# Eight gated cross-attention and feed-forward layers on one core: the last stage's experts on seven full tiles instead of eight short ones, two rounds sooner

## The chip, the cores and the metric

One core of one Trainium2 chip runs the whole program in one launch. The metric is device time in microseconds (us), the median of several executions. Engines are called TensorE (PE in the profile, PEld for its weight loads), VectorE (DVE), ScalarE (ACT), GpSimd (POOL) and SyncE (SP).

## What is computed

The reference is a stack of four layers, each a gated cross-attention and a gated feed-forward on x, which has 8 sequences of 112 rows of 1024 values. Only the last layer's two parts bear on the change:

```
idx = top_k(-pdist, 16)                      # 16 nearest of 1024 points, per sequence
gathered = take_along_axis(feat, idx)        # feat: layer norm of x, (1024 points, 112 rows)
x = x + tanh(g_xattn[3]) * (einsum('bkm,k->bm', gathered, affine_w) + affine_b)
# experts, row by row
p = softmax(layernorm(x) @ gate_w.T)         # 8 experts, the best two kept and made to sum to 1
x = x + tanh(g_ffn[3]) * sum_e w[e] * (layernorm(x) @ lora_A[e].T @ lora_B[e].T)
```

The experts treat each row by itself, so rows may be grouped in any way. The gather works on one sequence at a time and needs all its rows.

## The kernel before

The function `gather_experts` (L2829) is the last stage. It starts at about 2477 us. It is written as one list of rounds, `u` from 0 to 161 (`ROUNDS`, L2843). All four compute engines walk the same list in program order, so a wait in one round holds back all later rounds of that engine. A sequence b has 16 rounds, u = 16b to 16b+15, and k is the round's place in it.

In each round VectorE makes a one-hot matrix (`marked(u + 2)`, L3090, two rounds ahead), TensorE multiplies it with the table of the sequence (`looked`, L2938, 24 small matmuls at L2947), and VectorE reduces the result (`kept`, L3098, L3105). Three one-hot buffers and three banks of the look-up tie the two engines together within about three rounds. Every four rounds TensorE turns four results (`turned`, L2951) and ScalarE copies them to `flat` (L3017). Round k = 13 makes the next sequence's table (`tabled`, `split`), rounds 2 to 6 its layer norm.

The results of sequence b then take a path through memory to be regrouped. In round 16(b+1)+1 ScalarE stores `flat` (L3024, 448 KB); in round 16(b+1)+5 ScalarE waits for that store and issues the load into `back` (`back_load`, L3026, 448 KB). In the round that `returns` names (L2882: 16(b+1)+9, for b = 0 16(b+1)+11) TensorE waits for the load and turns the values (`returned`, L2960, L2966). Two rounds later VectorE adds them to x (`update`, L3109, L3114).

The experts of sequence m are 22 steps t, step t in round 16(m+1)+12+t (`steps`, L2877; for m = 0 the first five steps lie in rounds 30 to 32). t = 0 to 3 is the layer norm, t = 5 turns the rows (L2983, L675), t = 7 to 10 are the gate and the first product (L2973, with `zT`: 16 instructions of 128x8 and 16 of 128x512), t = 10 and 11 the weights and h on VectorE, t = 13 turns h, t = 15 to 18 are the second product (L2973, with `hT`, 16 of 128x512), t = 18 and 20 add it to x (L3165), t = 21 stores the rows (L3051). These steps handle 112 rows at a time. All lie in the same rounds as the gather of later sequences; only the last sequence's have nothing beside them.

The queues: SyncE loads the broadcast numbers of the next sequences (L298, 912 KB and 72 KB per piece, four pieces a sequence), each piece as soon as the buffer's rounds are consumed. ScalarE issues all other transfers of the stage: loads of x (L3058, round k = 0), `flat`, `back` and the output. GpSimd does one iota (L2925) and nothing else. Its DMAs are the software_dynamic queue of the profile.

Of the kernel before, what the change touches and what calls it, by code (L numbers as in the profile page):

```python
# [15 lines left out]
U32 = mybir.dt.uint32  # L16
# [2812 lines left out]
def gather_experts(nc, C, banks, gate, gate_ffn, x_in, x_out, A, gather, early):  # L2829
# [13 lines left out]
    ROUNDS = U + 12 + 22  # L2843
    with ExitStack() as ctx:
# [7 lines left out]
        norm = Norm(s_, 4)  # L2852
        shift = s_.sb("shift", [Q, 4, 1])
# [7 lines left out]
        zm, zT = s_.sb("zm", [Q, D]), s_.sb("zT", [P, KC, Q])  # L2861
        prob, best, w8, hit = (s_.sb(n, [Q, NE]) for n in ("prob", "best", "w8", "hit"))
        place, placef, number = s_.sb("place", [Q, 8], U32), s_.sb("placef", [Q, 8]), s_.sb("number", [Q, NE])
        nmax, both = s_.sb("nmax", [Q, 1]), s_.sb("both", [Q, 1])
        h, hT = s_.sb("h", [Q, RE]), s_.sb("hT", [P, RE // P, Q])
# [9 lines left out]
            s_.sem(n) for n in ("zm_ready", "zT_ready", "max_ready", "prob_ready", "h_ready", "hT_ready", "x_done"))  # L2875

        def steps(u):  # L2877
# [8 lines left out]
        order, nth = [], {}  # L2886
        for u in range(ROUNDS):
# [9 lines left out]
            if k == 2 and b + 1 < B:  # L2897
                nth["points", b + 1] = len(nth)
            for m, t in steps(u):
                if t == 0:  # L2900
                    nth["experts", m] = len(nth)
# [11 lines left out]

        @block.sync
        def _(sp):
            sp.wait_ge(x_loaded[2], 16)
            for b in range(1, B):
                for c in range(4):
                    if b >= 2:
                        sp.wait_ge(onehot_ready, (b - 2) * K + 4 * (c + 1))  # L2920
                    gather.load_spread(sp, b, c, spread_loaded[b % 2][c], spread[b % 2])

        @block.gpsimd
        def _(pool):
            pool.iota(number[:], pattern=[[1, NE]], base=0, channel_multiplier=0,  # L2925
                      allow_small_or_imprecise_dtypes=True).then_inc(numbered, 1)

        @block.tensor
        def _(pe):
# [39 lines left out]
            def part_of(t, lhsT, w, ks, n):  # L2969
                if ks[0] == 0:  # L2970
                    pe.wait_ge(turns.free(t), turns.count(t, 0))
                for k in ks:
                    mm = pe.matmul(turns.tile(t)[0:Q, 0:n], lhsT[:, k, :], w(k), start=(k == 0), stop=(k == lhsT.shape[1] - 1))  # L2973
# [3 lines left out]
            def experts(m, t):  # L2977
                if t == 5:
                    if m == 0:
                        pe.wait_ge(early.loaded["gT"], 16)  # L2980
                        pe.wait_ge(gather.weights_loaded, 32)
                    pe.wait_ge(zm_ready, m + 1)
                    turn_rows(pe, C, turns, zm, "zT", m, 0)  # L2983
                if t == 7:
                    pe.wait_ge(zT_ready, m + 1)
# [3 lines left out]
                if t == 13:  # L2989
                    pe.wait_ge(h_ready, m + 1)  # L2990
                    turn_rows(pe, C, turns, h, "hT", m, 0, n=1)
                if t == 15:
                    pe.wait_ge(hT_ready, m + 1)
# [19 lines left out]
        def _(act):  # L3013
            def turned(i):
                t = ("turn", i)
                act.wait_ge(turns.full(t), turns.count(t, 0))
                op = act.activation(flat[:, i // 4 % 2, :, i % 4 * 4:i % 4 * 4 + 4],  # L3017
# [8 lines left out]
            def back_load(b):  # L3026
                act.wait_ge(flat_stored, 16 * b + 16)
                act.dma_start(back[:, b % 2].rearrange("p t f -> p (t f)"),
                              flat_dram[b % 2].rearrange("a c -> (a c)").rearrange("(p c) -> p c", p=P)).then_inc(back_loaded[b % 2], 16)

            def scaled(out, src, i, n, ready):
                act.wait_ge(shift_ready, n + 1)
# [274 lines left out]
```

## Time and profile before

| what | us |
|---|---|
| three runs | 2803.63, 2813.75, 2813.39 (median 2813.39) |
| the profiled execution, its own time | 2815.97 |
| its span, first to last instruction | 2814.3 |
| TensorE busy in the span, from the page | 2584.0 (92%) |
| last stage, from its first look-up at 2477.5 to the end | 336.8 |
| granted clock of TensorE, mean over the span | 0.962 of full speed |

The rows of the trace name a line, an engine, what is written and read, how often, and times in us. A stretch A:B is counted from the span's start. For the last stage two kinds of moments are used as marks below: T_b is when ScalarE issues the store of `flat` of sequence b (2503.91, 2538.12, 2580.22, 2617.76, 2655.56, 2693.13, 2729.39 and 2762.68 for b = 0 to 7), and R_b is when TensorE begins to turn the returned values of b (2520.68, 2559.63, 2598.95, 2636.49, 2673.98, 2710.57, 2746.93 and 2776.40).

### The profile page before, as it was taken

How to read it: one execution, taken by the hardware profiler on the slowest of the kernel's cores; microseconds unless marked ns; L12 is line 12 of the kernel's file. 1: busy time of each engine (PE TensorE's matmuls, PEld its weight loads, DVE VectorE, ACT ScalarE, POOL GpSimd, SP SyncE). 2: the span in 40 equal slices, each digit the busy share in tenths (PEclk: the TensorE clock that was granted, in tenths of full speed). 3: DMA queues.
4: the chain of work that ended last, by engine and by line, in shares of the span. 5: the costliest groups of instructions: out<-in, count | busy, mean ns of one | idle time of the engine just before them, and what ended most of it. 6: DMA issues, size and time to landing. Idle time of an engine off the chain costs nothing. (4 is left out here: it accounts for less than half of the span.)

```text
span 2814.3 us, 48289 instructions
## 1 busy us (share of the span) xinstructions
PE 2584.0 (92%) x18264; PEld 1841.8 (65%) x18268; DVE 1898.8 (67%) x3366; ACT 1080.5 (38%) x2605; POOL 553.1 (20%) x602
## 2 busy tenths in 40 slices
PE   7999999999999699998899999998788999878898
PEld 5856855855865488886555555655487788556664
DVE  6376376376467577774578877777558889867774
ACT  3443434334335233332334444443355655302221
POOL 0110100001012100000045554455223333200000
PEclk9999999999999899998899999998899999989998
DMA  8011010101113845556275666544250010544521
GB/s 325 2 38 58 3 59 23 38 25 58 37 47 82 278 115 140 157 149 220 103 246 165 180 172 172 161 127 118 63 201 9 24 47 24 141 142 169 176 98 33
DMA packets 155491, 311.31 MB, mean 111 GB/s; under 512 B 84112, under 2 KB 107312, under 8 KB 145768
## 3 DMA queue, kind: packets, MB, share of 16 engines
q1 hardware_dynamic: 128952, 232.78, 25.8%
q0 software_dynamic: 20384, 60.82, 7.3%
q10 hardware_dynamic: 5936, 14.75, 1.8%
q8 instruction: 141, 2.31, 0.4%
q14 instruction: 78, 0.64, 0.1%
HBM read 249.53 MB, written 42.52 MB: 104 GB/s over the span
## 5 line engine op out<-in xcount | busy, mean ns | idle before, releaser
L1765 DVE TENSOR_REDUCE latent_nmax<-bank 112x1 f32<-112x487 f32 x128 | 85.0, 665 | 242.9 <-PE bank L1568 236.5
L1460 POOL TENSOR_SCALAR latent_probs<-latent_probs,latent_rsum 112x487 f32<-112x487 f32 x128 | 89.0, 709 | 786.0 <-DVE latent_rsum L1770 786.0
L2197 POOL TENSOR_SCALAR grouped_probs<-grouped_probs,grouped_rsum 112x375 f32<-112x375 f32 x256 | 169.8, 682 | 280.5 <-DVE grouped_rsum L2253 280.4
L2464 PE MATMUL bank<-ffn_qT,gather_whole 128*128 128x128 bf16 x3584 | 207.0, 220 | 16.7 <-ACT ffn_us L2587 6.7
L2464 PEld LDWEIGHTS bank<-ffn_qT,gather_whole 128*128 128x128 fp8e4 x3584 | 203.0, 98 | 21.6 <-issue 20.3
L2647 POOL TENSOR_TENSOR ffn_h<-ffn_sl,ffn_us 128x512 f32<-128x512 f32 x56 | 126.8, 2265 | 278.6 <-ACTq L2590 278.6
L2144 ACT ACTIVATE grouped_probs<-bank,grouped_nmax 112x375 f32<-112x375 f32 x256 | 143.3, 572 | 76.0 <-DVE grouped_nmax L2249 76.0
L2249 DVE TENSOR_REDUCE grouped_nmax<-bank 112x1 f32<-112x375 f32 x256 | 122.3, 540 | 73.4 <-PE bank L2055 71.1
L2947 PEld LDWEIGHTS bank<-gather_part,points_onehot 123*128 123x128 bf16 x3072 | 109.2, 101 | 60.9 <-DVE points_onehot L3095 30.8
L2064 PEld LDWEIGHTS bank<-const_ident,grouped_probs 112*125 112x125 f32 x768 | 105.4, 196 | 66.4 <-DVE grouped_probsT L2261 28.8
L2191 POOL TENSOR_SCALAR grouped_raw<-grouped_raw,grouped_rscale 128x1024 f32<-128x1024 f32 x96 | 119.9, 1270 | 144.7 <-DVEq L2227 144.5
L1515 PE MATMUL bank<-latent_zT,front_wq 128*128 128x224 f32 x768 | 148.0, 353 | 0.0
L1540 PE MATMUL bank<-latent_wo,latent_oT 128*128 128x512 f32 x336 | 146.6, 592 | 0.0
L1515 PEld LDWEIGHTS bank<-latent_zT,front_wq 128*128 128x128 f32 x768 | 145.0, 190 | 1.9 <-issue 1.8
L2947 PE MATMUL bank<-gather_part,points_onehot 123*128 123x63 bf16 x3072 | 115.2, 198 | 27.7 <-DVE points_onehot L3095 24.3
L2064 PE MATMUL bank<-const_ident,grouped_probs 112*125 112x112 f32 x768 | 110.2, 283 | 23.7 <-DVE grouped_probsT L2261 18.8
L1475 PE MATMUL bank<-front_wkv,front_cT 128*125 128x384 f32 x384 | 127.3, 492 | 0.0
L1475 PE MATMUL bank<-front_cT,front_wkv 128*128 128x375 f32 x384 | 123.3, 478 | 0.0
L1700 ACT ACTIVATE latent_probs<-bank,latent_nmax 112x487 f32<-112x487 f32 x128 | 85.5, 668 | 91.2 <-DVE latent_nmax L1765 80.9
L2580 ACT ACTIVATE ffn_sl<-ffn_gs,ffn_sgu 128x128 f32<-128x128 f32 x224 | 71.6, 390 | 116.5 <-DVEq L2710 116.0
L1527 PE MATMUL bank<-latent_probsT,latent_v 125*96 125x224 f32 (+1 forms) x512 | 110.1, 358 | 4.0 <-DVEq L1784 4.0
L1540 PEld LDWEIGHTS bank<-latent_wo,latent_oT 128*128 128x128 f32 x336 | 63.2, 190 | 73.9 <-issue 73.7
(435 smaller groups left out, 5561.7 us busy)
## 6 DMA issues: line engine op xcount, KB each, us to landing
grouped_raw<-L_weights SPq DMA_DIRECT2D x24, 2048.0 KB, 8.9
points_spread<-numbers SPq DMA_DIRECT2D x16, 912.0 KB
codes<-grouped_flip SPq DMA_DIRECT2D x24, 512.0 KB, 2.6
front_cT<-ctxT SPq DMA_DIRECT2D x8, 1500.0 KB, 6.8
plain_ctxT<-ctxT POOLq DMA_DIRECT2D x8, 1500.0 KB, 22.2
plain_ctx<-ctx POOLq DMA_DIRECT2D x8, 1500.0 KB, 23.5
grouped_ctx<-ctxT SPq DMA_DIRECT2D x8, 1500.0 KB, 6.8
gather_whole<-numbers SPq DMA_DIRECT2D x12, 912.0 KB
```

What stands on the lines that cost most here:

```text
L1475: mm = pe.matmul(turns.tile(t)[0:m, 0:n], lhsT(k), rhs(k), start=(k == 0), stop=(k == KC - 1))
L1515: mm = pe.matmul(turns.tile(t)[:, c * 2 * Q:(c + 1) * 2 * Q], wq[:, k, (2 * i + c) * P:(2 * i + c + 1) * P], zT[:, k].rearrange("p s q -> ...
L1527: mm = pe.matmul(turns.tile(t)[0:HD, 2 * half * Q:2 * (half + 1) * Q], v[0:n, k, g * HD:(g + 1) * HD], pT[0:n, half, k], start=(k == 0), s ...
L1540: mm = pe.matmul(turns.tile(t)[:], oT[:, (b - 1) % 2, k, :], wo[:, k, i * 512:(i + 1) * 512], start=(k == 0), stop=(k == OC - 1))
L2064: mm = pe.transpose(turns.tile(t)[0:CT, j * Q:(j + 1) * Q], pr[:, g % 2, j, k * CT:(k + 1) * CT], C.ident[0:Q, 0:Q])
L2144: act.activation(pr[:, i, j, :], turns.tile(t)[0:Q, 0:CTX], ACT.Exp, bias=nmax[:, i, j:j + 1], accum_out=rsum[:, i, j:j + 1]).then_inc(tur ...
L2191: pool.tensor_scalar(w, w, rscale[:, slot, i % m:i % m + 1], MAGIC, ALU.mult, ALU.add).then_inc(raw_scaled, 1)
L2197: pool.tensor_scalar(pr[:, g % 2, j, :], pr[:, g % 2, j, :], rsum[:, g % 2, j:j + 1], 1.0, ALU.mult, ALU.mult)\
L2249: dve.tensor_reduce(nmax[:, g % 2, j:j + 1], turns.tile(t)[0:Q, 0:CTX], AX, ALU.max, negate=True).then_inc(max_ready, 1)
L2464: mm = pe.matmul(ahead.tile(t)[:, i * P:(i + 1) * P], wgu[:, u0 + f // 4, c:c + 2 * P - 1:2], qT[:, k, :], start=(k == 0), stop=(k == KC - 1))
L2647: pool.tensor_tensor(h[:, G * j:G * j + G, :], sl[:, j % 2], us[:, j % 2], ALU.mult).then_inc(h_ready, 1)
L2947: mm = pe.matmul(turns.tile(t)[:, j * RA:(j + 1) * RA], onehot[0:ROWS, u % 3, j * P:(j + 1) * P], part[n][0:ROWS, b % 2, :], start=(n == 0 ...
```

## The change

Sequences 1 to 7 have 112 rows each, on partitions 0 to 111 of their tile. The 112 rows of sequence 0 are cut into seven parts of 16, and each part is copied onto partitions 112 to 127 of one of these tiles (`full[m]`). The experts run for m = 1 to 7 on 128 rows; m = 0 has none. `returns` goes from round 16(b+1)+9 to 16(b+1)+7 (b = 0 stays at +11), the experts from 16(m+1)+12+t to 16(m+1)+10+t. The load of `back` goes from ScalarE's queue to GpSimd's, where it stands in no round but behind the store of `flat` alone. GpSimd also copies the seven parts (after `update(0)`, semaphore `first_done`; VectorE waits for them, `rows_moved`, in step 0 of m = 1) and stores the 16 extra rows of each tile, the last one excepted, which SyncE stores.

```diff
-    ROUNDS = U + 12 + 22
+    ROUNDS = U + 10 + 22
-        rest_x, z = s_.sb("x", [Q, B - 1, D]), s_.sb("z", [Q, 2, NA * CH])
-        x = [early.sb["x0"][:]] + [rest_x[:, b, :] for b in range(B - 1)]
+        rest_x, z = s_.sb("x", [P, B - 1, D]), s_.sb("z", [Q, 2, NA * CH])
+        x = [early.sb["x0"][:]] + [rest_x[0:Q, b, :] for b in range(B - 1)]
+        full = [None] + [rest_x[:, b, :] for b in range(B - 1)]
...
-            return [(m, t) for m in range(B) for t in range(22)
-                    if u == ((30, 30, 31, 31, 32)[t] if m == 0 and t < 5 else 16 * (m + 1) + 12 + t)]
+            return [(m, t) for m in range(1, B) for t in range(22) if u == 16 * (m + 1) + 10 + t]
...
-            return [m for m in range(B) if u == 16 * (m + 1) + (11 if m == 0 else 9)]
+            return [m for m in range(B) if u == 16 * (m + 1) + (11 if m == 0 else 7)]
...
+        def back_load(eng, b):
+            eng.wait_ge(flat_stored, 16 * b + 16)
+            eng.dma_start(back[:, b % 2].rearrange("p t f -> p (t f)"),
+                          flat_dram[b % 2].rearrange("a c -> (a c)").rearrange("(p c) -> p c", p=P)).then_inc(back_loaded[b % 2], 16)
+
+        def store_first(eng, m, stored):
+            eng.dma_start(x_out[0][(P - Q) * (m - 1):(P - Q) * m], full[m][Q:P]).then_inc(stored, 16)
...
+            sp.wait_ge(x_done, B - 1)
+            store_first(sp, B - 1, x_stored)
...
+            back_load(pool, 0)
+            pool.wait_ge(first_done, 1)
+            for m in range(1, B):
+                pool.dma_start(full[m][Q:P], x[0][(P - Q) * (m - 1):(P - Q) * m]).then_inc(rows_moved, 16)
+            for b in range(1, B):
+                back_load(pool, b)
+                if b >= 3:
+                    pool.wait_ge(x_done, b - 2)
+                    store_first(pool, b - 2, rows_stored)
+            pool.wait_ge(x_done, B - 2)
+            store_first(pool, B - 2, rows_stored)
+            pool.wait_ge(rows_stored, 16 * (B - 2))
...
+                if i % 4 == 0 and i >= 8:
+                    act.wait_ge(flat_stored, 16 * (i // 4 - 1))
...
-                if k == 5 and 1 <= b <= B:
-                    back_load(b - 1)
...
-                dve.drain()
+                if b == 0:
+                    dve.drain().then_inc(first_done, 1)
+                else:
+                    dve.drain()
...
+                    if m == 1:
+                        dve.wait_ge(rows_moved, 16 * (B - 1))
+                    wide.statistics(dve, full[m], i)
```

The rest of the diff widens the experts' tiles from 112 to 128 partitions, gives them a layer-norm workspace of their own (`wide`), and lowers the counts of their semaphores by one, as m starts at 1.

## Rows read from the trace of the kernel before

**Rows 1.** Busy time by stretch of the last stage, last: granted clock, DMA, GB/s.

```profile
core 0: us, PE busy (x) PEld busy (x) DVE busy (x) ACT busy (x) POOL busy (x), PEclk, DMA share, GB/s
2477.50:2503.91 26.41, 20.60 (x490) 19.05 (x490) 22.38 (x48) 3.81 (x6) 0.00 (x0) 0.92 0.54 176
2503.91:2520.68 16.77, 9.94 (x224) 8.92 (x224) 13.98 (x29) 2.63 (x4) 0.00 (x0) 0.86 0.53 181
2520.68:2538.12 17.44, 13.83 (x181) 12.42 (x182) 10.95 (x24) 2.60 (x4) 0.00 (x0) 0.60 0.43 155
2538.12:2559.63 21.51, 16.81 (x240) 12.02 (x239) 14.82 (x39) 5.27 (x8) 0.00 (x0) 0.90 0.51 170
2559.63:2580.22 20.59, 19.44 (x250) 14.63 (x250) 13.28 (x28) 4.34 (x6) 0.00 (x0) 0.90 0.44 149
2580.22:2598.95 18.73, 16.07 (x236) 11.31 (x236) 14.04 (x38) 5.15 (x8) 0.00 (x0) 1.00 0.55 193
2598.95:2617.76 18.81, 17.62 (x250) 12.87 (x250) 15.13 (x32) 4.34 (x6) 0.00 (x0) 1.00 0.46 152
...
2655.56:2673.98 18.42, 16.07 (x236) 11.32 (x236) 13.73 (x38) 5.15 (x8) 0.00 (x0) 1.00 0.58 197
...
2693.13:2710.57 17.44, 15.75 (x237) 11.26 (x237) 12.99 (x36) 4.56 (x7) 0.00 (x0) 1.00 0.38 134
...
2762.68:2776.40 13.72, 11.96 (x34) 6.31 (x33) 2.36 (x14) 2.53 (x4) 0.00 (x0) 0.75 0.39 102
2776.40:2814.30 37.90, 29.48 (x89) 13.87 (x87) 10.58 (x28) 6.35 (x9) 0.00 (x0) 0.89 0.08 24
```

**Rows 2.** The chain of waits, last stage: start us, us, what.

```profile
2503.91 7.41 DMA flat<-points_flat
2511.34 9.30 DMA points_back<-flat
...
2538.12 10.73 DMA flat<-points_flat
2548.87 10.72 DMA points_back<-flat
...
2589.91 9.00 DMA points_back<-flat
...
2764.53 12.03 PE bank L2973 x32
```

**Rows 3.** Groups of instructions in the last stage (busy us, mean ns | idle before).

```profile
L2973 PE MATMUL bank<-gather_whole,points_zT 128*112 128x512 f32 x128 | 65.6, 646 | 0.0
L2973 PE MATMUL bank<-gather_whole,points_hT 128*112 128x512 f32 x128 | 61.0, 606 | 1.3 <-ACTq L686 1.3
```

**Rows 4.** Timeline of VectorE: one plain round, from mark to mark.

```profile
2503.60 0.49 DVE L3095 TENSOR_SCALAR points_onehot<-points_spread,points_consts 123x1024 bf16<-123x1024 bf16 x1
...
2504.82 0.48 DVE L3095 TENSOR_SCALAR points_onehot<-points_spread,points_consts 123x1024 bf16<-123x1024 bf16 x1
```

**Rows 5.** Timeline of ScalarE: its issues of the load of back.

```profile
2665.24 0.34 ACTq L3028 DMA_DIRECT2D points_back<-flat  x1
...
2767.34 0.34 ACTq L3028 DMA_DIRECT2D points_back<-flat  x1
```

**Rows 6.** DMA issues: KB each, median us from issue to landing.

```profile
gather_whole<-numbers POOLq DMA_DIRECT2D x4, 912.0 KB, 14.0
...
front_x<-front_cT POOLq DMA_DIRECT2D x1, 512.0 KB, 10.1
...
points_x<-x SPq DMA_DIRECT2D x1, 448.0 KB, 5.2
...
scales<-grouped_scale SPq DMA_DIRECT2D x24, 2.0 KB, 3.0
...
mem_gw<-L_ffn_gate_w POOLq DMA_DIRECT2D x1, 0.5 KB, 5.2
```

**Rows 7.** Timeline of TensorE at R_1, in brackets its idle time before.

```profile
2559.63 1.96 PE L2966 MATMUL bank<-const_ident,points_back 128*112 128x128 f32 x8 [3.60 <-DMA points_back<-flat]
```

More of the change, by code:

```diff
@@ L2860, in gather_experts @@
         gT, aT, bT = early.sb["gT"], gather.aT, gather.bT
[L2861 to L2865, printed above, removed]
+        zm, zT = s_.sb("zm", [P, D]), s_.sb("zT", [P, KC, P])
+        prob, best, w8, hit = (s_.sb(n, [P, NE]) for n in ("prob", "best", "w8", "hit"))
+        place, placef, number = s_.sb("place", [P, 8], U32), s_.sb("placef", [P, 8]), s_.sb("number", [P, NE])
+        nmax, both = s_.sb("nmax", [P, 1]), s_.sb("both", [P, 1])
+        h, hT = s_.sb("h", [P, RE]), s_.sb("hT", [P, RE // P, P])
         numbered = s_.sem("numbered")
@@ L2972, in part_of @@
                 for k in ks:
-                    mm = pe.matmul(turns.tile(t)[0:Q, 0:n], lhsT[:, k, :], w(k), start=(k == 0), stop=(k == lhsT.shape[1] - 1))
+                    mm = pe.matmul(turns.tile(t)[0:P, 0:n], lhsT[:, k, :], w(k), start=(k == 0), stop=(k == lhsT.shape[1] - 1))
                 if ks[-1] == lhsT.shape[1] - 1:
@@ L2989, in experts @@
                 if t == 13:
-                    pe.wait_ge(h_ready, m + 1)
-                    turn_rows(pe, C, turns, h, "hT", m, 0, n=1)
+                    pe.wait_ge(h_ready, m)
+                    turn_rows(pe, C, turns, h, "hT", m, 0, n=1, rows=P)
                 if t == 15:
-                    pe.wait_ge(hT_ready, m + 1)
+                    pe.wait_ge(hT_ready, m)
                 if 15 <= t < 19:
@@ L3024, in turned @@
                     act.dma_start(flat_dram[b % 2], flat[:, b % 2].rearrange("a n k -> a (n k)")).then_inc(flat_stored, 16)
[L3026 to L3032, printed above, removed]
-                act.activation(out, src, ACT.Identity, bias=shift[:, i, :], scale=norm.rstd[:, i, :]).then_inc(ready, 1)
             def experts(m, t):
-                i, n = 2 + m % 2, nth["experts", m]
+                i = m % 2
                 if t == 0:
-                    norm.root(act, i, n)
+                    wide.root(act, i, m - 1)
                 if t == 3:
-                    scaled(zm[:], x[m], i, n, zm_ready)
+                    act.wait_ge(wide_shift_ready, m)
+                    act.activation(zm[:], full[m], ACT.Identity, bias=wide_shift[:, i, :], scale=wide.rstd[:, i, :]).then_inc(zm_ready, 1)
                 if t == 6:
-                    copy_turned(act, turns, zT, "zT", m, 0, zT_ready)
+                    copy_turned(act, turns, zT, "zT", m, 0, zT_ready, rows=P)
                 if t == 9:
-                    act.wait_ge(max_ready, m + 1)
-                    act.activation(prob[:], turns.tile(("gate", m))[0:Q, 0:NE], ACT.Exp, bias=nmax[:]).then_inc(turns.free(("gate", m)), 1)
+                    act.wait_ge(max_ready, m)
+                    act.activation(prob[:], turns.tile(("gate", m))[0:P, 0:NE], ACT.Exp, bias=nmax[:]).then_inc(turns.free(("gate", m)), 1)
                     act.drain().then_inc(prob_ready, 1)
                 if t == 14:
-                    copy_turned(act, turns, hT, "hT", m, 0, hT_ready, n=1)
+                    copy_turned(act, turns, hT, "hT", m, 0, hT_ready, n=1, rows=P)
                 if t == 21:
-                    act.wait_ge(x_done, m + 1)
+                    act.wait_ge(x_done, m)
                     act.dma_start(x_out[m], x[m]).then_inc(x_stored, 16)
@@ L3134, in weighed @@
                 dve.drain()
-                dve.tensor_scalar(best[:, 0:2], best[:, 0:2], both[:], C.gates[0:Q, gate_ffn:gate_ffn + 1], ALU.mult, ALU.mult)
+                dve.tensor_scalar(best[:, 0:2], best[:, 0:2], both[:], C.gates[:, gate_ffn:gate_ffn + 1], ALU.mult, ALU.mult)
                 dve.drain()
@@ L3151, in experts @@
                     dve.wait_ge(turns.full(g), turns.count(g, 0))
[L3152 removed]
+                    dve.tensor_reduce(nmax[:], turns.tile(g)[0:P, 0:NE], AX, ALU.max, negate=True).then_inc(max_ready, 1)
                 if t == 10:
@@ L3164, in experts @@
                     dve.wait_ge(turns.full(g), turns.count(g, 0))
-                    dve.tensor_tensor(x[m][:, c], turns.tile(g)[0:Q, :], x[m][:, c], ALU.add).then_inc(turns.free(g), 1)
+                    dve.tensor_tensor(full[m][:, c], turns.tile(g)[0:P, :], full[m][:, c], ALU.add).then_inc(turns.free(g), 1)
                     if t == 20:
```

47 lines of the change are left out of this document (21 added, 26 removed).

## The prediction

> **What bounds the kernel now.** I began with the page: TensorE is the busiest engine, but that is an average over eight parts of the program. The change touches the last stage alone, so I went to the stretches between the marks T_b and R_b [rows 1]. From T_b to R_b the values of sequence b travel through memory; from R_b to the next T the rest of the period runs. Then the chain of waits [rows 2] says what ended each stretch. For b = 0 and b = 1 the whole way from T to R is two transfers back to back, 7.41 + 9.30 and 10.73 + 10.72 us. TensorE is not the limit there: it waits, and as it works through its rounds in order, everything behind waits too. For b = 2 the load is still in the chain (9.00 us), but it had been issued 9.69 us after T by the place of its round. So T to R is a matter of memory for b = 0 to 4 (16.8, 21.5, 18.7, 18.7, 18.4 us), and R to T a matter of TensorE: 17.62 of 18.81 us busy for b = 2. Only for b = 5 and 6, where SyncE has finished its loads of numbers, does TensorE arrive last.
>
> **The change, part by part.**
>
> *One expert pass less.* It has 16 instructions of each of the two large groups: (65.6 + 61.0) / 8 = 15.8 us of TensorE [rows 3]. All of it lay in the period T_1 to T_2 (42.1 us). Its first product lies between T_1 and R_1, under the two transfers; removed, TensorE only waits longer. Its second product lies between R_1 and T_2, 20.59 us. Without it I compose that stretch from the one for b = 0, which has no products: 17.44 us for six rounds after R_0. After the change ten rounds follow R_1. A plain round of VectorE takes 2504.82 - 2503.60 = 1.22 us [rows 4], so 17.44 + 4 x 1.22 = 22.3 us, **+1.7** us. The pass is worth nothing here: the wait and the two rounds more take its place.
>
> *Two rounds sooner.* The values are wanted six rounds after T instead of eight; the memory path doesn't get shorter. What was done in these two rounds during the flight now comes after R. For b = 2, 3, 4 that is 2 x 1.22 = 2.44 us each, **+7.3** us. Bounds: 1 us each if they fit into VectorE's gaps, 2.7 with the turning of the experts' rows. For b = 5 and 6 the values are there in time and the steps only change places; I put **-1.0** us for both, as the experts' work spreads a little better (bounds -2 and +1).
>
> *The store's start.* T_b itself keeps its place. But x_out of the previous tile used to be issued behind the store of `flat` and now goes ahead of it by three rounds, from b = 3 on: 448 KB in the same queue. I take +1.5 us each for b = 3 and 4, with bounds 0 and 4.7, the time in which the last store was through (2767.34 - 2762.68) [rows 5].
>
> *The load from GpSimd.* It goes out when the store has landed, not at ScalarE's round 5. For b = 0 and 1 ScalarE already waited for it: nothing to gain. For b = 2 and 3 it was issued 9.7 us after T; the store took between 7.4 and 9.7, I take 8.6: gain 1.1 each. For b = 4: 2665.24 - 2655.56 = 9.7 [rows 5], with no load of x ahead of the store, I take 7: gain 2.7. Against that stands the price of a DMA that GpSimd issues. Small transfers took 5.2 us from GpSimd and 3.0 from SyncE [rows 6]: 2.2 us more, which I take. The bounds are 0 and 4.9 (512 KB in 10.1 us from GpSimd, 448 KB in 5.2 from SyncE; the first also adds, so it is high). T to R thus changes by +2.2, +2.2, +1.1, +2.6 and +1.0 us for b = 0 to 4: **+9.1** us, less 1.2 because the load no longer queues behind x_out on ScalarE's queue for b = 2 and 3: **+7.9**.
>
> The Trainium skill (DMA: Bandwidth & Descriptors, Specifications) gives a first-byte latency of about 1 us for GpSimd's path and 0.6 for the other. As an estimate from that page the surcharge is 0.4 us a load and the sum would be 9 us smaller; the row on small transfers disagrees, and I follow the row.
>
> *The clock.* After the wait of 3.6 us before R_1 [rows 7] the granted clock was 0.90 in the next stretch, 20.59 us; for b = 2 with a short wait it was 1.00, 18.81 us [rows 1]. Both have the same rounds and products, so the fall from 2.4 to 1.2 GHz costs up to 1.8 us after a long wait. The waits of b = 2 and 3 become about 5 us long (TensorE reaches R some 15 us after T, the values come at 20 to 21). As two plain rounds more stand behind R, which VectorE sets, I take half: **+1.8** us for both, bounds 0 and 5.4 for three.
>
> *128 rows instead of 112.* The large products stream 512 columns as before. Turning and copying grow by a seventh, some 0.1 us on the path at each place, hidden but for the tail. GpSimd's seven copies (64 KB each) start after `update(0)` and are wanted 13 rounds later; cover gone, each microsecond would count. The 16-row stores run beside others; the last lies beside the 112-row store. I put **0**.
>
> *The tail.* Before, the first product of m = 6 (12.03 us, partly at 1.2 GHz [rows 2], clock 0.75 [rows 1]) began 1.9 us after T_7 and held back R_7 until 13.7 us after T_7. Now its rows are turned before the last look-up, so it starts about 2.5 us sooner. The values come after the store, 4.7 us, and a load: between 3.0 (a small transfer [rows 6]) and 4.7 (a store of the same size), I take 3.4, and 2.2 for GpSimd: 10.3 us. So R_7 falls 3.4 us sooner, bounded by 2 and 4.4. From R_7 to the end (37.90 us) it is one expert pass in a line, as before: **-3.4**.
>
> Sum: 1.7 + 7.3 - 1.0 + 7.9 + 1.8 - 3.4 = **+14.3** us. The profiled execution took 2815.97 us, 2.6 above the median of 2813.39; all terms are differences of its stretches, so I add them to the median of the runs: 2827.7, say **2827.5 us**.
>
> **The rivals.**
>
> *A, not slower: the path is short enough.* Mechanism: the load on a queue of its own, freed from ScalarE's round and from x_out, lands as early as TensorE now asks, so nothing is lost behind R. For: ScalarE was up to 2.7 us late. Against: T to R of b = 1 is 21.5 us of pure transfer, with six rounds before it. It decides if store and load together stay under 16 us. Then only b = 0, the tail and small terms are left: +2.2 + 1.7 - 3.4 - 2 = about -1, so 2812 us.
>
> *B, faster: TensorE's work counts.* If values of b = 1 came within 8 us, the period T_1 to T_2 would run like the first 26.4 us, which hold 17 rounds without an expert [rows 1]: 42.1 - 26.4 = 15.7 us less, with the tail 19: 2794 us. Against it stand the two transfers of 10.7 us.
>
> *C, much slower: GpSimd's loads starve.* Mechanism: GpSimd must write each load's descriptors itself while VectorE works. A row shows 14.0 us for 912 KB from GpSimd beside a busy VectorE [rows 6]. If a load of 448 KB takes 14 instead of 9 us, each of the five costs 2.8 us more than I took: +14, in all 2842 us. It decides where the load's landing time passes 12 us. The Trainium skill (SBUF — State Buffer, SBUF: two separate sides) names such a trap: descriptor writing stops while VectorE runs in a two-port mode. By that rule the one-hot marks, 0.49 of each 1.22 us, would be the cause; no row before shows a load of `back` on this queue.
>
> **How the numbers follow.** A measurement here can tell 0.5% from no change, about 14 us. The forecast, waits longer and rounds moved behind them, has a chance of 0.60; A 0.17, B 0.10, C 0.13. The forecast's own range, with bounds combined, goes from 2809 (no surcharge, no clock loss, the rounds half absorbed) to 2840. With A inside at 2812 and half of C, the range is **2807 to 2842**. My sum lies on the border of 0.5%: of the forecast a little over half is slower by more than that. Slower 0.34 + 0.13 = 0.47, same 0.26 + 0.17 = 0.43, faster 0.10.
>
> **What would show it.** In the changed profile: TensorE's idle time ended by the load of `back` before R_b grows to 5 us and more for b = 2 and 3, and to over 10 us for b = 1. T_1 to R_1 stays at 21 us or more and R_1 to T_2 at 21 us or more with TensorE busy for much less. T to R for b = 2, 3 is 19 us or more, R to T 21 us. The load's time from issue to landing is 10 to 12 us instead of about 9. Low clock appears between 2600 and 2660. R_7 comes 10 to 11 us after T_7. I am wrong if the landing falls to 7 us, or T to R below 16 us, or if b = 5 and 6, which I hold unchanged, move by over 2 us.

## The result, and the profile of the changed kernel

The changed kernel took a median of 2820.67 us over 20 runs (2812.34 to 2834.34), the kernel before 2813.55 on the same chips (20 runs, 2803.63 to 2817.93). The ratio, taken round by round, is **1.0028, interval 1.0017 to 1.0039**: some 8 us slower, which lies within 0.5%. The profiled execution took 2817.85 us (span 2816.2), 2.8 us below its median, where that of before lay 2.4 above: the spans differ by 1.9 us only. The last stage, which the change touches alone, grew by more: 336.8 us before, 2816.2 - 2471.9 = 344.3 now, **+7.5** (what lies ahead of it was 5.6 us shorter in this execution, with the same code). So I compare stretches of the stage.

Busy time by stretch after, between the same marks (T_b, R_b) as in [rows 1]; the columns are those of [rows 1]:

```profile
2498.34:2514.34 16.00, 9.94 (x224) 8.93 (x224) 12.53 (x27) 2.63 (x4) 0.58 (x1) 0.87 0.53 184
2514.34:2532.70 18.36, 15.88 (x196) 14.95 (x197) 11.01 (x21) 1.18 (x2) 3.39 (x7) 0.50 0.56 142
2532.70:2548.79 16.09, 7.44 (x135) 6.84 (x132) 8.84 (x19) 2.03 (x3) 0.57 (x1) 0.61 0.52 178
2548.79:2571.12 22.33, 19.06 (x295) 18.55 (x295) 15.10 (x32) 4.41 (x7) 0.00 (x0) 0.72 0.45 159
2571.12:2585.74 14.62, 13.11 (x173) 8.66 (x173) 9.81 (x31) 2.93 (x5) 0.55 (x1) 1.00 0.54 191
2585.74:2610.06 24.32, 22.28 (x315) 17.68 (x316) 20.32 (x41) 6.73 (x10) 0.00 (x0) 0.93 0.49 177
2610.06:2628.84 18.78, 12.99 (x174) 8.54 (x173) 11.50 (x33) 3.59 (x5) 1.03 (x2) 0.93 0.50 176
2628.84:2654.97 26.13, 24.07 (x315) 19.50 (x316) 17.35 (x35) 6.18 (x9) 0.00 (x0) 0.85 0.44 169
2654.97:2670.57 15.60, 13.11 (x173) 8.65 (x173) 9.81 (x31) 3.58 (x5) 1.06 (x2) 1.00 0.54 190
2670.57:2694.94 24.37, 22.33 (x315) 17.80 (x316) 18.62 (x38) 6.07 (x9) 0.00 (x0) 0.93 0.42 163
...
2765.97:2777.36 11.39, 11.39 (x27) 5.87 (x28) 2.36 (x14) 1.55 (x2) 1.06 (x2) 0.70 0.30 89
2777.36:2816.20 38.84, 29.94 (x89) 15.00 (x87) 10.60 (x28) 6.56 (x9) 0.49 (x1) 0.88 0.09 27
```

Rows come in pairs, T_b to R_b and R_b to the next T. The second of each pair grew everywhere: 24.32 us for b = 2 where [rows 1] has 18.81, and 26.13 for b = 3. The first shrank: 16.09 us for b = 1 (before 21.51), 14.62 for b = 2 (18.73). Only b = 3 has 18.78. The clock, which was 1.00 in both stretches of b = 2, is 0.93 and 0.85 in R_2 to T_3 and R_3 to T_4.

The chain of waits after, as in [rows 2]; two sequences:

```profile
2610.06 9.76 DMA flat<-points_flat
2620.11 8.69 DMA points_back<-flat
...
2654.97 7.16 DMA flat<-points_flat
2662.41 8.12 DMA points_back<-flat
```

As before, store and load stand back to back. The load is through in 8.69 and 8.12 us, not in 10 to 12. The DMA issues of the stage give its median, 7.8 us (from ScalarE's queue it was 8.8):

```profile
points_back<-flat POOLq DMA_DIRECT2D x8, 448.0 KB, 7.8
```

TensorE's timeline at R_3 (in brackets its idle time and what ended it), as in [rows 7]:

```profile
2622.89 0.87 PE L2966 MATMUL bank<-gather_part,points_onehot 123*128 123x63 bf16 x24 [0.72 <-DVE points_onehot L3105]
2628.84 1.96 PE L2985 MATMUL bank<-const_ident,points_back 128*112 128x128 f32 x8 [5.07 <-DMA points_back<-flat]
2630.59 1.06 PE L675 MATMUL bank<-const_ident,points_h 128*128 128x128 f32 x4
```

The wait of 5.07 us is there. At R_1 it was 5.52, at R_0 2.82, at R_4 1.82, but at R_2 only 0.83.

| b | 0 | 1 | 2 | 3 | 4 | 5 | 6 |
|---|---|---|---|---|---|---|---|
| T to R, before / after | 16.8 / 16.0 | 21.5 / 16.1 | 18.7 / 14.6 | 18.7 / 18.8 | 18.4 / 15.6 | 17.4 / 13.8 | 17.5 / 13.6 |
| R to T, before / after | 17.4 / 18.4 | 20.6 / 22.3 | 18.8 / 24.3 | 19.1 / 26.1 | 19.2 / 24.4 | 18.8 / 23.7 | 15.8 / 19.9 |

### The profile page after: what moved, and what is told of

It reads as the page before. It is cut to its first block and busy times, and to the rows that moved or that the text cites. A ratio compares the mean times of both kernels' runs of the same rounds, so it can differ in the third digit from the quotient of the medians.

```text
span 2816.2 us, 48140 instructions
## 1 busy us (share of the span) xinstructions
PE 2581.9 (92%) x18208; PEld 1849.5 (66%) x18208; DVE 1892.0 (67%) x3343; ACT 1075.8 (38%) x2597; POOL 563.3 (20%) x623
## 5 line engine op out<-in xcount | busy, mean ns | idle before, releaser
L2464 PE MATMUL bank<-ffn_qT,gather_whole 128*128 128x128 bf16 x3584 | 206.9, 220 | 16.7 <-ACT ffn_us L2587 6.7
L2464 PEld LDWEIGHTS bank<-ffn_qT,gather_whole 128*128 128x128 fp8e4 x3584 | 202.9, 98 | 21.7 <-issue 20.3
L2966 PEld LDWEIGHTS bank<-gather_part,points_onehot 123*128 123x128 bf16 x3072 | 117.8, 105 | 55.1 <-DVE points_onehot L3105 28.5
L2966 PE MATMUL bank<-gather_part,points_onehot 123*128 123x63 bf16 x3072 | 123.2, 203 | 26.9 <-DVE points_onehot L3105 23.8
L3115 DVE TENSOR_REDUCE points_val<-bank 128x56 f32<-128x504 f32 x128 | 86.9, 679 | 45.7 <-PE bank L2966 45.4
```

The source lines that it names most:

```text
L2464: mm = pe.matmul(ahead.tile(t)[:, i * P:(i + 1) * P], wgu[:, u0 + f // 4, c:c + 2 * P - 1:2], qT[:, k, :], start=(k == 0), stop=(k == KC - 1))
L2966: mm = pe.matmul(turns.tile(t)[:, j * RA:(j + 1) * RA], onehot[0:ROWS, u % 3, j * P:(j + 1) * P], part[n][0:ROWS, b % 2, :], start=(n == 0 ...
```

## The experiments

Edits are to the changed kernel unless said otherwise. Each ratio is to the kernel before, in brackets its interval; 1.0028 is the change itself. "Stage" is the profiled last stage (before 336.8, after 344.3 us); it is one execution, and its end alone moves it: R_7 to the end took 34.5 to 35.5 us in the traces in which the clock there was 0.95 to 0.97, and 37.9 to 38.9 in those with 0.88 or 0.89. So the medians of the runs decide, and of a trace its single stretches are read.

**One part at a time.** Seven tiles and GpSimd's load, at the old places:

```diff
-    ROUNDS = U + 10 + 22
+    ROUNDS = U + 12 + 22
-            return [(m, t) for m in range(1, B) for t in range(22) if u == 16 * (m + 1) + 10 + t]
+            return [(m, t) for m in range(1, B) for t in range(22) if u == 16 * (m + 1) + 12 + t]
-            return [m for m in range(B) if u == 16 * (m + 1) + (11 if m == 0 else 7)]
+            return [m for m in range(B) if u == 16 * (m + 1) + (11 if m == 0 else 9)]
```

> The kernel after with the rounds put back: returned values turned at +9, experts at +12 as before; seven tiles and the loads on GpSimd stay. Theory 'too soon' (the time is lost because the values are asked for two rounds early): 7 to 14 us faster than the kernel after, so between 0 and 7 us faster than the kernel before; T to R for b = 2 to 4 is 16 to 18 us with hardly a wait, R to T 19 us. Theory 'GpSimd's queue is slow' (2.2 us or more a load): still 4 us or more slower than before. Theory 'the pass of sequence 0 costs or gives nothing': within 2 us of the kernel with eight tiles and loads on GpSimd.

Measured: 0.9968 (0.9952 to 0.9984), 2806.93 us, stage 327.7. TensorE waits for no value from b = 1 on. Against the change this is 1.0060, some 17 us (7 to 14 had been expected), and the two rounds are all that differs.

Then the kernel before with all eight passes at the sooner places (the pass of sequence 0 only one round sooner, as its values allow no more):

```diff
-    ROUNDS = U + 12 + 22
+    ROUNDS = U + 10 + 22
-                    if u == ((30, 30, 31, 31, 32)[t] if m == 0 and t < 5 else 16 * (m + 1) + 12 + t)]
+                    if u == ((30, 30, 31, 31, 31)[t] if m == 0 and t < 5 else 16 * (m + 1) + (11 if m == 0 else 10) + t)]
-            return [m for m in range(B) if u == 16 * (m + 1) + (11 if m == 0 else 9)]
+            return [m for m in range(B) if u == 16 * (m + 1) + (11 if m == 0 else 7)]
```

> The kernel before with eight tiles and ScalarE's loads, but values and experts two rounds sooner (m = 0 one round sooner, as far as its data allow). Theory 'too soon': slower than before by 10 us or more, as ScalarE's load goes out only at round 5 and lands 9 us later, with TensorE asking at round 7. Theory 'the seven tiles cost' (copies, 128 rows): at most 3 us slower than before.

Measured: 1.0077 (1.0054 to 1.0101), 2833.06 us, stage 357.7. The two rounds cost some 22 us here, and 17 in the company of the other two parts. T_1 to R_1 was 21.7 us and T_2 to R_2 24.3, with waits of 5.81 and 6.71 us. For b = 3 to 6 T to R was 14.2 to 14.5 us with waits under 1 us: the loss is in the first three periods.

The kernel before with the load alone moved to GpSimd (ScalarE then waits for the store itself before it writes into `flat` again):

```diff
...
-                if k == 5 and 1 <= b <= B:
-                    back_load(b - 1)
...
+                if i % 4 == 0 and i >= 8:
+                    act.wait_ge(flat_stored, 16 * (i // 4 - 1))
...
+            for b in range(B):
+                pool.wait_ge(flat_stored, 16 * b + 16)
+                pool.dma_start(back[:, b % 2].rearrange("p t f -> p (t f)"),
+                               flat_dram[b % 2].rearrange("a c -> (a c)").rearrange("(p c) -> p c", p=P)).then_inc(back_loaded[b % 2], 16)
```

> The kernel before with the load of back on GpSimd's queue and nothing else. The forecast's surcharge of 2.2 us a load: T to R grows by 2 us for b = 0 and 1, in all 2 to 5 us slower. Theory 'no surcharge' (the load lands 8 us after its issue, as in the trace after): T to R shrinks or stays, in all 0 to 5 us faster, limited because TensorE waited only about 1 us for b = 2 to 4 and 3.6 us for b = 0 and 1.

Measured: 0.9971 (0.9955 to 0.9986), 2802.96 us, stage 327.0. The load's move is worth some 8 us **by itself**. A surcharge as forecast would have made it 2 to 5 us slower. It is as good as the first experiment, which has seven passes: 0.9968 against 0.9971. The eighth pass, together with the seven copies and the wider rows that replace it, is worth nothing that these runs can tell. The stretches T_1 to R_1 and R_1 to T_2 show where its work went. Busy time by stretch, with eight passes (load on GpSimd):

```profile
2533.12:2552.24 19.12, 16.40 (x241) 11.65 (x239) 13.43 (x37) 5.24 (x8) 0.56 (x1) 0.98 0.54 179
2552.24:2570.96 18.72, 17.56 (x250) 12.79 (x250) 14.71 (x31) 4.34 (x6) 0.00 (x0) 1.00 0.45 165
```

and with seven, at the old places:

```profile
2538.51:2555.46 16.95, 9.55 (x188) 8.57 (x185) 9.11 (x20) 2.12 (x4) 0.58 (x1) 0.70 0.52 175
2555.46:2576.37 20.91, 15.75 (x232) 14.68 (x233) 15.42 (x33) 3.03 (x5) 0.00 (x0) 0.67 0.45 164
```

TensorE was busy for 16.40 + 17.56 = 34.0 us in the one and 9.55 + 15.75 = 25.3 in the other, and the period is 37.84 and 37.86 us. The granted clock is 0.98 and 1.00 with the pass, 0.70 and 0.67 without it: a good part of it ran at 1.2 GHz. But the clock is not what holds this period. The waits of VectorE from T_1 to T_2 with seven passes (engine, what it waited with, for what: us in total, times, longest us):

```profile
DVE points_onehot L3105 <- DMA gather_whole<-numbers: 10.6, 3, 6.3
```

VectorE waited 10.6 us for SyncE's loads of numbers, and TensorE for VectorE's marks; with eight passes it waited for them not once in this period. The period can't end before the numbers are there. e11_late_small below is the same kernel with these loads cut, and its period T_1 to T_2 is 28.3 us.

The change with the load back in ScalarE's round 5:

```diff
...
-                back_load(pool, b)
...
+                if k == 5 and 1 <= b <= B:
+                    back_load(act, b - 1)
```

> The kernel after with the load of back put back on ScalarE's queue at round 5. Forecast's surcharge: 5 to 9 us faster than after. Theory 'no surcharge, ScalarE's place is late': slower than after by 5 us or more, because the load goes out at round 5 or later and TensorE asks at round 7; waits before R of 4 us and more for b = 1 to 4 and low clock behind them.

Measured: 1.0049 (1.0032 to 1.0066), 2826.74 us, stage 352.1. T to R was 21.5 and 21.3 us for b = 2 and 3, with 7.75 and 7.63 us of waiting there, as groups of waits in that stretch say (us in total, times, longest us):

```profile
PE bank L2983 <- DMA points_back<-flat: 15.4, 2, 7.7
```

With six rounds ahead of R, ScalarE's round 5 comes 11.5 us after T, where GpSimd issued it after 6.9 to 10.1. So GpSimd gives back some 6 us of what the rounds cost. There is no surcharge to be seen. (The wait of 4 us and more that had been expected for b = 4 as well was 0.87.)

**Why the rounds behind R grew by so much.** I had a rival: that the layer norm and table of the next sequence (rounds 2 to 14) now met the experts' steps badly. They were moved two rounds sooner as well (in this order: statistics, root, shifted rows, z, and the table; its splitting likewise):

```diff
-                if k == 2 and b + 1 < B:
+                if k == 0 and b + 1 < B:
...
-                if k == 3 and b + 1 < B:
+                if k == 1 and b + 1 < B:
...
-                if k == 5 and b + 1 < B:
+                if k == 3 and b + 1 < B:
...
-                if k == 6 and b + 1 < B:
+                if k == 4 and b + 1 < B:
...
-                if k == 13 and b + 1 < B:
+                if k == (13 if b < 2 else 11) and b + 1 < B:
```

> The kernel after with the next sequence's layer norm and table two rounds sooner as well (statistics at round 0, root 1, shift 3, z 4; table at 11 and split at 12 from the third sequence on), so that everything but the looks keeps its old distance to the experts. Theory 'alignment' (R to T grew by 4 to 5 us instead of 2.4 because TensorE's block of gate and first product now stands where VectorE has nothing beside it, and the table falls on the last addition): 1 to 2 us less in each of the periods of b = 2 to 6, in all 5 to 9 us faster than after. Rival 'only waits and clock': unchanged within 2 us.

Measured: 1.0031 (1.0017 to 1.0045), 2822.08 us. R to T stayed as it was, 24.4, 26.6 and 24.4 us for b = 2 to 4. That rival fell: 5 to 9 us had been expected of it.

The clock's share was to be told by four matmuls of 512 columns on data at hand, issued before the waits at R_1 and R_3:

```diff
+                if b in (1, 3):
+                    pe.wait_ge(gather.weights_loaded, 32)
+                    pe.wait_ge(turns.free(("back", b, 0)), turns.count(("back", b, 0), 0))
+                    for j in range(4):
+                        pe.matmul(turns.tile(("back", b, 0))[:, 0:512], C.ident[:], aT[:, j, :], start=True, stop=True)
                 pe.wait_ge(back_loaded[b % 2], b // 2 * 16 + 16)
```

> The kernel after with four matrix products more (identity by the first weights, 512 columns, their result is overwritten) on TensorE just before it waits for the returned values of b = 1 and b = 3, the two waits of over 5 us. Theory 'clock' (a long wait costs on top of itself because the clock falls behind it): the low clock behind R_1 and R_3 disappears or shrinks, R to T of b = 1 and 3 falls by 1 to 2 us each, 2 to 4 us faster than after. Rival 'VectorE sets the pace there, the clock is for nothing': unchanged or up to 1 us slower.

Measured: 1.0026 (1.0004 to 1.0047), 2822.54 us. In its trace R_3 to T_4 went from 26.1 to 24.2 us, which would be the clock's 2 us, but the median didn't move, and this trace lies 10 us below its own median. R_2 to T_3, where nothing had been added, fell as well, from 24.3 to 22.8, with the clock at 1.00 instead of 0.93 and the same wait before it (0.89 and 0.83 us). So these four products are not shown to be the reason. What a low clock costs in such a stretch can be read across the traces, as R to T holds the same 315 matmuls each time: 22.7 to 23.0 us at 1.00 (22.75 in e6_warm and 22.74 in e7_queue, both b = 2), 24.2 to 24.4 at 0.93, 25.9 to 26.8 at 0.84 to 0.87. What it costs the median isn't resolved.

Next the transfers that lie beside the path: the load of x and the store of the output were issued behind the store of `flat` instead of ahead of it.

```diff
-                if k == 0 and b + 3 < B:
+                if k == 2 and b + 3 < B:
                     act.dma_start(x[b + 3], x_in[b + 3]).then_inc(x_loaded[b + 3], 16)
...
-                if t == 21:
+                if t == (21 if m == B - 1 else 23):
...
```

> The kernel after with two transfers of ScalarE's queue moved behind the store of flat: the load of x from round 0 to round 2, the store of the finished rows from step 21 to step 23 (round 1, after flat). Theory 'the store queues behind them' (forecast: 1.5 us for b = 3 and 4, bounds 0 and 4.7): T to the landing of the store falls from 10.1 to about 6 us for b = 3, from 8.1 and 6.9 to 6 for b = 1 and 2; T to R by as much; with less wait 4 to 8 us faster than after. Rival 'SyncE's loads of numbers slow the store': the store still takes 8 us or more for b = 3, unchanged within 2 us.

Measured: 1.0000 (0.9984 to 1.0017), 2812.87 us: 8 us better than the change. T_3 to the load's issue fell from 10.1 to 8.2 us, T_3 to R_3 from 18.8 to 16.7; but over b = 1 to 4 the time from T to the load's issue hardly changed in sum (32.5 and 32.1 us), so the path gives only a part of the gain. The stage of this trace is 8.8 us shorter than after, and 6.6 of them lie behind T_7, where the clock was 1.00 and 0.95 instead of 0.70 and 0.88. e5_shift and e6_warm had that same quick end without a better median, so where the median's 8 us come from stays open.

To see how much of the growth is waiting for memory, SyncE's loads of numbers were cut, for the third sequence on, from 1024 to 64 columns. That leaves most of the look-up's numbers of these sequences out, so the gathered values are not the reference's:

```diff
-                    gather.load_spread(sp, b, c, spread_loaded[b % 2][c], spread[b % 2])
+                    if b == 1:
+                        gather.load_spread(sp, b, c, spread_loaded[1][c], spread[1])
+                        continue
+                    for w, r0, n in ((0, 0, 114), (1, 114, 9)):
+                        sp.dma_start(spread[b % 2][r0:r0 + n, c, 0:64], gather.numbers[b, w, 32 * c:32 * c + 1, 0:64]
+                                     .broadcast_to([n, 64])).then_inc(spread_loaded[b % 2][c], 16)
```

> The kernel after, with SyncE's loads of numbers for the third and later sequences cut to 64 columns of each row (the one-hot matrices of these sequences are then built from other numbers, so their gathered values are not the reference's; every instruction of the compute engines stays). Theory 'SyncE's loads slow store and load of back': T to the store's landing 4 to 5 us and from there to R under 6 us for b = 2 to 4, TensorE never waits for back from b = 2 on, 6 to 10 us faster than after. Rival 'the path is long by itself': T to R of b = 3 stays above 16 us.

Measured: 0.9941 (0.9921 to 0.9962), 2796.42 us, stage 320.2, some 24 us better than the change where 6 to 10 had been expected; the DMA issues give

```profile
points_back<-flat POOLq DMA_DIRECT2D x8, 448.0 KB, 3.5
```

3.5 us for the load, 7.8 after: **more than half of each transfer on the path was contention** with SyncE's stream (the store went from 7 to 10 us down to 4, from b = 1 on). Busy time by stretch, T_1 to R_1 to T_2 and T_3 to R_3 to T_4:

```profile
2529.06:2536.69 7.63, 4.90 (x136) 4.32 (x133) 6.18 (x14) 1.18 (x3) 0.57 (x1) 0.98 0.43 125
2536.69:2559.47 22.78, 18.46 (x295) 17.87 (x295) 17.37 (x37) 5.16 (x8) 0.00 (x0) 0.70 0.09 24
2598.35:2611.96 13.61, 12.88 (x174) 8.55 (x174) 7.88 (x26) 2.35 (x4) 1.03 (x2) 1.00 0.26 74
2611.96:2635.63 23.67, 21.05 (x321) 16.07 (x317) 20.21 (x42) 7.32 (x10) 0.00 (x0) 1.00 0.08 23
```

T_1 to R_1 is 7.63 us, and the period T_1 to T_2 30.4 where it was 38.4 after. VectorE waits for no numbers any more. With b = 3 TensorE doesn't wait for the values: 13.61 us ahead of R and 23.67 behind it, 37.3 together. So the sooner place costs behind R about what it saves ahead of it, if the values are there.

The same cut, with the places of the first experiment:

> The first experiment (values at +9, experts at +12) with the same cut of SyncE's loads. As TensorE hardly waited for back there, it gains at most 2 us from the cut. Theory 'only the waits make two rounds sooner dear': this kernel and the previous one lie within 2 us of each other, as neither waits from b = 2 on. Rival 'two rounds sooner costs also without waits' (the profile after shows 1.2 us more in the period of b = 5, where nothing waits): this one is 4 us or more faster than the previous.

Measured: 0.9923 (0.9903 to 0.9943), 2792.18 us, stage 317.1. Not 2 us at most came of the cut here but some 13 (0.9968 to 0.9923), though TensorE had hardly waited for values. Busy time by stretch, T_1 to R_1 to T_2:

```profile
2531.63:2541.68 10.05, 6.76 (x187) 6.10 (x185) 8.43 (x19) 2.04 (x3) 0.58 (x1) 1.00 0.35 97
2541.68:2559.89 18.21, 14.02 (x237) 13.05 (x236) 15.63 (x34) 3.11 (x5) 0.00 (x0) 0.72 0.11 29
```

The period went from 37.86 to 28.26 us, 9.6 less, about what VectorE had waited for numbers. The clock behind R_1 is as low as before (0.72), so it was not the clock that had made this period as long as with the pass. Eight passes kept TensorE busy for 34.0 us of it: by that estimate the pass taken out would be worth at least 5.7 us here, were the numbers in time. By the ratios the two rounds cost some 5 us without SyncE's stream (0.9941 against 0.9923, with intervals that overlap) and 17 with it.

**Other places.** With the values of sequence 0 at +15 instead of +11 and the rest at the old places:

```diff
...
-            return [m for m in range(B) if u == 16 * (m + 1) + (11 if m == 0 else 7)]
+            return [m for m in range(B) if u == 16 * (m + 1) + (15 if m == 0 else 9)]
```

> Seven tiles, loads on GpSimd, experts at +12 and returned values at +9 (the first experiment), and in addition the values of b = 0 turned at +15 instead of +11. Seven tiles allow that: no expert waits for sequence 0 before round 44. Theory: TensorE's wait of 3.4 us before R_0 goes, with the low clock behind it: period of b = 0 from 32.8 to 30 us or less, 3 to 5 us faster than the first experiment, so 12 to 14 us faster than the kernel before. Rival: the wait only moves to the table or to b = 1: within 1 us of the first experiment.

Measured: 0.9961 (0.9946 to 0.9976), 2803.37 us. The wait at R_0 vanished, and one of 5.96 us stood at R_1: the wait had only moved. The interval overlaps that of the first experiment, on which 3 to 5 us had been expected.

One round sooner instead of two:

```diff
...
-            return [(m, t) for m in range(1, B) for t in range(22) if u == 16 * (m + 1) + 10 + t]
+            return [(m, t) for m in range(1, B) for t in range(22) if u == 16 * (m + 1) + 11 + t]
...
-            return [m for m in range(B) if u == 16 * (m + 1) + (11 if m == 0 else 7)]
+            return [m for m in range(B) if u == 16 * (m + 1) + (11 if m == 0 else 8)]
```

> Half of the move: seven tiles, loads on GpSimd, values at +8 and experts at +11 (the kernel after has +7 and +10, the first experiment +9 and +12). Theory 'threshold' (the move costs once TensorE asks before the load lands, some 16 us after T, and it reaches +8 about 15.7 us after T): close to the first experiment, 0.996 to 0.999 of the kernel before, waits of under 1.5 us before R_2 to R_4. Rival 'each round sooner costs the same': half way, 0.9998, with R to T about 2.5 us longer per period but T to R 1.8 us shorter, no wait needed.

Measured: 1.0105 (1.0086 to 1.0125), 2842.49 us, stage 364.3: **slower than both neighbours**, 0.9968 at the old places and 1.0028 at two rounds sooner. Both theories, with at most 0.9998, missed it. From b = 2 on nothing waits for memory, yet the periods of b = 2 to 5 are 41 to 45 us. The timeline of all engines behind T_4 (the last line from TensorE's own):

```profile
2661.51 0.59 ACT L3038 ACTIVATE points_flat<-bank 56x512 f32<-56x512 f32 x1 [6.83 <-PE bank L2975]
...
2662.21 0.32 ACTq L3045 DMA_DIRECT2D flat<-points_flat  x1
2662.57 1.09 ACT L684 ACTIVATE points_zT<-bank 128x512 f32<-128x512 f32 x2 [0.47 <-ACTq L3043]
...
2663.75 2.52 PE L2992 MATMUL bank<-points_gT,points_zT 128*128 128x8 f32 x16 [1.55 <-ACTq L686]
...
2666.13 3.76 PE L2992 MATMUL bank<-gather_whole,points_zT 128*128 128x512 f32 x4
```

At this place the experts' step 6, in which ScalarE copies `zT`, falls in round 1, where it stands in program order behind the copy into `flat` and its store (L3038, L3045). TensorE waits 1.55 us for it (L686). The four products that follow take 3.76 us. With the old places TensorE's timeline has the same four in 1.96:

```profile
2653.23 1.96 PE L2992 MATMUL bank<-gather_whole,points_zT 128*128 128x512 f32 x4
```

So ScalarE was asked, in this last kernel, to take the experts' step first in that round:

```diff
+                if k == 1:
+                    for m, t in steps(u):
+                        experts(m, t)
                 if k % 4 == 1 and 1 < u <= U + 1:
                     turned(u // 4 - 1)
...
-                for m, t in steps(u):
+                for m, t in steps(u) if k != 1 else []:
```

> The kernel with values at +8 and experts at +11, and on ScalarE in round 1 the expert's step (the copy of the turned rows, which frees TensorE's gate products) ahead of the copy and store of flat instead of behind them. Theory 'a queue of its own making' (in the +8 kernel TensorE waits 1.5 us for that copy in each period, its clock falls, and the first product runs at half speed: T to R 18 to 20 us with no wait for memory, clock 0.83): T to R back to about 16 us for b = 2 to 6 with the clock at 1.00, 20 to 30 us faster than the +8 kernel, 0.997 to 1.002 of the kernel before. Rival 'the +8 place is bad for other reasons' (VectorE's last addition behind the table, R to T 23 us): T to R falls by 1.5 us a period at most, still 1.006 or more.

Measured: 1.0039 (1.0019 to 1.0060), 2824.55 us, stage 347.8: 18 us given back by the order of two steps on one engine in one round (20 to 30, and at most 1.002, had been expected). Busy time by stretch, T_4 to R_4, with the copy of `zT` behind the one into `flat`:

```profile
2662.21:2682.12 19.91, 17.15 (x180) 11.44 (x181) 9.86 (x31) 4.67 (x7) 1.06 (x2) 0.83 0.51 182
```

and ahead of it:

```profile
2659.82:2675.95 16.13, 13.83 (x181) 9.39 (x180) 10.59 (x32) 3.59 (x5) 1.06 (x2) 1.00 0.54 179
```

The granted clock there was 0.83 and is 1.00 now: the four products no longer run at 1.2 GHz. What is left over the old places lies behind R: 24.7, 26.8, 24.9 and 23.2 us for b = 2 to 5 against 18.9 there, of which T to R gives back 0.4 to 2.6. There are waits for memory too, 6.96 us at R_1 and 2.40 at R_3, but the change has 5.52 and 5.07.

## Why the prediction was right and wrong

The direction and the order of size were right (+14.3 forecast; +7.9 measured by the ratio, +7.5 in the stage); this came of two terms that were wrong in opposite directions, which is luck.

| term | forecast | in the two profiles |
|---|---|---|
| R_1 to T_2, the pass less | +1.7 | +1.7 |
| T to R, b = 0 to 4 | +7.9 | -0.8 -5.4 -4.1 +0.1 -2.8 = -13.0 |
| R to T, b = 2, 3, 4, with the clock | 7.3 + 1.8 = +9.1 | +5.5 +7.1 +5.2 = +17.8 |
| R_0 to T_1 | 0 | +0.9 |
| b = 5 and 6, whole periods | -1.0 | +1.5 |
| tail | -3.4 | T_7 to R_7 -2.3, R_7 to the end +0.9: -1.4 |
| sum | +14.3 | +7.5 |

*The pass is worth nothing:* the number held, and e1_late against e3_pool8 shows it, 0.9968 and 0.9971. I had put it down to the path through memory and two rounds more. At the old places neither is at work, and there it is a third thing that I had overlooked: SyncE's loads of numbers, for which VectorE waited 10.6 us in that period. With them cut, it fell by 9.6 us. In the change itself VectorE waited 3.0 and 1.1 us for them around T_1, and TensorE 5.5 for the values. The stretch R_1 to T_2 came out as composed, 22.3 us, but partly by luck: without SyncE's stream two rounds more cost 4.6 us there (22.8 in e10_small, 18.2 in e11_late_small), not 2.4.

*T to R,* the step "Against that stands the price of a DMA that GpSimd issues", in which I took 2.2 us a load: **this step failed.** From the load's issue to R it was 8.8, 8.0, 7.7, 8.7 and 8.2 us for b = 0 to 4, before 9.3, 10.8, 9.0, 9.1 and 8.7. The row I took it from was a transfer of half a KB elsewhere in the program; the load of 448 KB shows none of it. The estimate from the first-byte latencies of the Trainium skill (DMA: Bandwidth & Descriptors, Specifications), 0.4 us, was the nearer one, and even that isn't seen. (The tail's load held the 2.2 us too, so by that estimate the sum would have been 10.8 us smaller and not 9.) The Trainium skill (DMA: Bandwidth & Descriptors, Issuing engines are not separate DMA queues) says that transfers of different issuers are interleaved on the same 16 engines, so another issuer gives no path of its own. The trace agrees: with SyncE's loads cut, the same load on the same queue took 3.5 us and not 7.8. What GpSimd gives is the moment of issue. It issued at 6.9 to 10.1 us after T where ScalarE's round now would have come at 11.5 (e4_act). And T_1 to R_1, which I held to be 21 us of pure transfer, fell by 5.4: store and load took 8.1 and 8.0 us, not 10.8 each. Seven tiles at the old places have 8.7 and 8.2, eight with the load on GpSimd 10.6 and 8.6: the load is quicker in both, the store only with seven tiles. Why the store is quicker wasn't tried.

*Two rounds sooner,* "A plain round of VectorE takes 1.22 us": **this step failed too,** and with it the clock's term. The stretches behind R hold experts' work beside the look-ups, and VectorE's plain round isn't their measure: R_2 to T_3 before is eight rounds in 18.81 us, 2.35 a round on average, so two are 4.7. Sequences 5 and 6, which wait for nothing, come near it: +4.9 and +4.1 behind R. It is no price of each round, though: with one round moved (e9_plus8, e12_copyfirst) R_5 to T_6 was already 23.2 us, against 18.9 with none and 23.7 with two. Why the first one costs so much stays open. Where the values are in time, T to R gives most of it back (-3.6 and -3.9): the two whole periods moved by +1.3 and +0.2 us, within the 2 us that I had allowed, though not to -1.0. The net loss is what the path does not let it give back: periods 2 to 4 took 38.9, 44.9 and 40.0 us against 36.0, 36.6 and 36.8 at the old places with seven tiles, 14.5 more; with SyncE's stream cut they took 38.9, 37.3 and 37.4, so 10.3 of the 14.5 went. The rest, 2.9 of it at b = 2, is of the places themselves and stays open.

*The longer waits:* half held. I had expected 5 us at R_2 and R_3 and over 10 at R_1; it was 0.83, 5.07 and 5.52. At b = 3 the store took 10.1 us, with the x load and x_out in the same queue ahead of it, as the step on the store's start had it; moving the two behind it took 1.9 us off, near the +1.5 I took for b = 3; for b = 4, where I had taken the same, the store was through in 7.4 us.

*The clock:* low stretches appeared where I said, between 2600 and 2660 (0.93 and 0.85). Their price was taken too low. With R to T at 22.74 us when the clock is 1.00 (e7_queue, b = 2), the +17.8 us behind R for b = 2 to 4 is +11.2 for the rounds, where I had 7.3, and +6.6 for the clock, where I had 1.8. The wait alone doesn't set it: before R_2 it was 0.83 us here and 0.89 in e6_warm, and behind it the clock was 0.93 and 1.00.

*The tail:* too good by 2 us, and not for the reason given. R_7 came 11.4 us after T_7, where I had 10.3 for a store and a load. But the store took 3.9 us, and TensorE did not wait for the load at R_7: it was busy with the product of m = 6 for all of the 11.4 us, at a clock of 0.70 (the line of T_7 to R_7 above). In e5_shift the same work took 8.0 us at 1.00:

```profile
2772.97:2781.00 8.03, 8.03 (x27) 4.15 (x28) 2.37 (x14) 1.55 (x2) 1.06 (x2) 1.00 0.44 127
```

So the product still held R_7, and its clock set the time; that the sum of the transfers came near was luck. The pass from R_7 on, on 128 rows, took 0.9 us longer, where I had put 0.

*Of the rivals,* A had T to R right: a load freed from its round lands soon enough for b = 2. It decided at 16 us for store and load, and b = 3 missed that; that nothing is then lost behind R was wrong. B, TensorE's work counts, has its condition met in e10_small: the values of b = 1 came within 7.6 us, and the period T_1 to T_2 was 30.4 us, 11.7 less than before, where B had 15.7. So it was the transfers, and SyncE's stream behind them, that kept the pass from paying. C, GpSimd's loads starving beside VectorE's marks, is shown by no run: 7.8 us beside the same marks.

What would beat both kernels: the old places with GpSimd's load, on eight tiles (0.9971), seven (0.9968), or seven with the first values later (0.9961). These three can't be told apart.

## What to carry to other kernels

A step that is moved in a static order is priced by what the rounds that it passes hold, on the engine that is busy there (+4.8 us for two rounds here, where VectorE's plain rounds said 2.4), and gives that back only where its data are already there; so shorten the path first (here the moment at which the load is issued), and only then ask for its result sooner. Price each step on every engine that holds it: one round of difference put an expert copy behind another copy in ScalarE's order, and that was worth 18 us. Before work is taken off an engine, look what else comes due in that stretch: here loads of numbers held the period as long as the work had. Where a wait for a transfer is on the path, count what else moves at that time before blaming the queue that issues it.

## What had not been expected of the hardware

Taking 8.7 us of work from TensorE in one period (34.0 to 25.3) brought no time, as loads of numbers came due there (10.6 us of waits); the granted clock fell along with it from 0.98 and 1.00 to 0.70 and 0.67. The same 315 matmuls between R and T took 22.7 to 23.0 us at a clock of 1.00, 24.2 to 24.4 at 0.93 and 25.9 to 26.8 at 0.84 to 0.87. A wait of 1.55 us in the midst of dense work was followed by the same four products in 3.76 instead of 1.96 us. A load of 448 KB took 3.5 us with the stream of SyncE cut and 7.8 beside it; from GpSimd it was no slower than from ScalarE (7.8 and 8.8 us in the two kernels).
